# Attention: TensorE takes the 64-row score products of two steps together, and the other pieces are placed anew

## The chip, the cores and the metric

The kernel runs on one core of one Trainium2 chip. The metric is the device time of one execution in microseconds, as the median of several runs. The engines are called as in the profile: PE (TensorE, matrix products), PEld (its weight loads), DVE (VectorE), ACT (ScalarE), POOL (GpSimd) and SP (SyncE, which issues DMAs).

## The reference, cut to what matters

The input is 8 batches of 512 tokens with 256 features. A layer of causal attention with 16 heads of 16 features and a layer of routed experts run on the same normalised input. A second layer follows. The change lies in the attention of the first layer and in the small pieces that are woven into it.

```python
xn = _layernorm(x, axis=-1)
qkv = jnp.einsum('bsd,hde->bhse', xn, Wqkv) + bqkv[None, :, None, :]
q, k, v = jnp.split(qkv, 3, axis=-1)
score = jnp.einsum('bhsd,bhtd->bhst', q, k)
score = jnp.where(causal[None, None], score, -jnp.inf)
attn = jax.nn.softmax(score / jnp.sqrt(HEAD_DIM), axis=-1)
y = jnp.einsum('bhst,bhtd->bhsd', attn, v)
out = transpose_and_reshape(y) @ Wout + bout
...
scores = jax.nn.softmax(xn @ gate_w.T, axis=-1)      # router: two of eight experts for each token
```

## The kernel before

`mix_phase` holds the attention, its projections and the router. It takes the first 480 us of the profiled span. Each engine runs a program of its own, written out in order, and the engines meet on semaphores only. All of them walk the same steps: 8 batches, 16 heads in each, `U = 3` steps in a head. This makes 48 steps in a batch and 384 in all. In the loops `s` is the head counted over all batches, `at` is the step within its batch (0 to 47), and `i` is the step within its group of four heads (0 to 11). A batch has four groups. Two steps that begin with an even number are called a pair below (0 and 1, 2 and 3, and so on).

What PE does in a step:

- `scores_k` (L996, L999, L1000) makes a third of the scores of the next head, with the keys as rows, in one of two PSUM banks. It waits until `exps` of ACT (L583) has read what stood in that bank two steps earlier. A contraction has 49 rows.
- `scores_q` (L972, then two mask products L976 and L977) makes scores with the queries as rows, two groups ahead, only to take their maxima. Its results go to three banks in turn. `maxima` of DVE (L798) reads them, one unit in each step, and unit `i` waits until the maxima of unit `i - 3` are taken. A contraction has 48 or 64 rows.
- Each of these two uses one half of the 128 rows of the array, and in a step they use opposite halves, so that they run at the same time.
- The other pieces use all 128 rows. `turn_maxima` (L982) transposes the maxima of a finished group. DVE copies them to `max_rows` (L805), ACT issues two small DMAs that bring them into `q_stack` (`send_max`, L598, at `AT_SEND`, i = 4), and the first `scores_k` of the next group, at i = 9, waits for them. `values` (L1014) multiplies the exponentials with V in three parts, `turn_out` (L1024) transposes the result, and `divide` of DVE (L775, L777) scales it. `x_transposes` (L895), `q_products`, `k_products`, `v_products` and `logits` (all in `three_products`, L154 to L156) prepare the next batch. `out_transposes` (L1034) and `out_products` (L154 to L156) finish the batch before. `rank_sums` (L949, L950) belongs to the router.

At which step a piece stands is written in tables: `AT_X_T`, `AT_OUT_T`, `Q_STEPS`, `K_STEPS`, `PROJ_STEPS`, `V_STEPS`, `AT_LOGITS`, `AT_VALUES`, `AT_TURN` for PE, and `AT_STATS`, `AT_NORM`, `AT_RANKS` and others for DVE and POOL. ACT and DVE take their part of a piece one or two steps after PE (`at - 1`, `at - 2`). DVE also does `norm_stats` (L658, L666), `normalise` (L676), `residual` (L789), `x_low` (L683), `k_low` (L687), `out_low` (L784), `v_bias` (L695) and the router's small steps (L716 to L766), all in one order with the maxima.

The rows of Q and K of the next batch make a round trip through memory: ACT, POOL and DVE write `qk_hi` and `qk_lo`, SP stores them (`store_slots`, L371) and loads the stacks when the stores have landed (`fetch_heads`, L400). The first half of the heads is needed by `scores_q` at step 24 of the batch before, the second half at step 0 of the batch itself. After the loop of batch 0, SP also issues one store of zeros of 4 MB (`y_routed_dram`, L436), behind `store_xn(2)`, which waits for the last `normalise` of that batch.

## Time and profile before

| | us |
|---|---|
| median of 3 runs | 1220.95 (1220.65 to 1225.09) |
| the profiled execution | 1231.83 |
| its span, from first to last instruction | 1230.1 |
| PE busy in it | 1122.1 |
| DVE busy in it | 898.4 |
| ACT busy in it | 685.9 |
| POOL busy in it | 522.9 |

The profiled execution is one of its own, 10.9 us above the median. Its span leaves out 1.7 us. Times of a stretch are read from it; differences are carried to the median as they are. Matrix products are pipelined. A row of PE gives when a product starts and a modelled end, and the distance from start to start is what it costs in a stream. Rows of a timeline merge equal instructions that follow each other.

### The profile page before, as it was taken

Reading aid. Unit: us, or ns where it says so; the run is one execution under the profiler, and the core shown is the slowest. Engines: PE = TensorE matmul, PEld = TensorE weight load, DVE = VectorE, ACT = ScalarE, POOL = GpSimd, SP = SyncE. Lnnn points to the kernel's source line nnn. Section 1 sums busy time; section 2 is a strip of 40 time slices with the busy share of each in tenths; the row PEclk is TensorE's granted clock in tenths of the full one; section 3 lists DMA queues with packets and bytes.
Section 4 is the critical chain, followed back from the end, with each engine's and each line's share of the span. In section 5 each row is a group of like instructions: output and inputs, shape, how many; then the busy total and the mean of one; then the engine's idle time right before and its main releaser. Section 6 shows DMA issues by size and latency. Waiting matters only on the chain. (4 is left out here: it accounts for less than half of the span.)

```text
span 1230.1 us, 27639 instructions
## 1 busy us (share of the span) xinstructions
PE 1122.1 (91%) x9352; PEld 730.6 (59%) x9353; DVE 898.4 (73%) x2247; ACT 685.9 (56%) x1463; POOL 522.9 (43%) x752
## 2 busy tenths in 40 slices
PE   3889889999899887999899999997999999999998
PEld 2444444445454433888799888885556556556555
DVE  4769688887988663887566676675877877877866
ACT  2256466565665462656565666664654654654653
POOL 6124234242432221946344344433447447447424
PEclk8589999999999887999899999998999999999999
DMA  5437433344533402666232444443232322322312
GB/s 155 117 79 226 109 104 91 101 109 102 117 88 87 105 18 66 190 215 186 85 128 81 118 122 142 148 135 105 99 90 74 113 82 78 114 77 81 99 35 69
DMA packets 105783, 133.60 MB, mean 109 GB/s; under 512 B 11616, under 2 KB 93472, under 8 KB 104672
## 3 DMA queue, kind: packets, MB, share of 16 engines
q1 hardware_dynamic: 97760, 113.47, 31.9%
q0 software_dynamic: 6912, 18.88, 5.5%
q8 instruction: 50, 0.82, 0.3%
q14 instruction: 37, 0.30, 0.1%
q10 hardware_dynamic: 1024, 0.13, 0.1%
HBM read 84.70 MB, written 47.58 MB: 108 GB/s over the span
## 5 line engine op out<-in xcount | busy, mean ns | idle before, releaser
L583 ACT ACTIVATE p<-bank 128x384 f32<-128x384 f32 (+1 forms) x384 | 196.5, 526 | 184.5 <-PE bank L996 125.2
L798 DVE TENSOR_REDUCE neg_max<-bank 128x1 f16<-128x512 f32 (+3 forms) x384 | 223.0, 598 | 76.7 <-PE bank L977 74.2
L473 POOL TENSOR_SCALAR_AFFINE_SELECT p<-p 128x256 f32<-128x256 f32 x256 | 104.5, 413 | 259.2 <-ACT p L583 256.9
L972 PE MATMUL bank<-k_stack,q_stack 48*128 48x384 f16 (+3 forms) x512 | 140.0, 324 | 15.2 <-DMA k_stack<-qk_dram 13.0
L1444 POOL DMA_INDIRECT fetched<-xn_dram,token_now x80 | 80.5, 1006 | 42.9 <-POOL token_now L1440 30.7
L1014 PE MATMUL bank<-p,v_aug 128*32 128x512 f32 (+3 forms) x1024 | 97.9, 481 | 0.8 <-DVE o_rows L777 0.8
L996 PE MATMUL bank<-q_stack,k_stack 49*128 49x512 f16 (+1 forms) x256 | 90.2, 379 | 8.3 <-DMA q_stack<-max_rows 6.6
L2084 POOL TENSOR_TENSOR he_lo<-he_sq,he_hi 128x512 f16<-128x512 f32 x64 | 79.9, 1269 | 36.6 <-ACT he_hi L2173 36.6
L2073 POOL TENSOR_TENSOR up_lo<-up_sq,up_hi 128x512 f16<-128x512 f32 x32 | 43.8, 1399 | 121.3 <-ACT up_hi L2130 121.3
L1528 ACT ACTIVATE a<-xbank,b 128x256 f32<-128x256 f32 (+1 forms) x126 | 58.6, 468 | 52.8 <-PE xbank L156 49.2
L1616 DVE TENSOR_TENSOR h_lo<-h,h_hi 128x256 f16<-128x256 f32 x159 | 67.9, 430 | 25.8 <-ACT h_hi L1537 25.0
L154 PE MATMUL ybank<-l_xT_hi,pack_hi 128*128 128x512 f16 x208 | 79.7, 383 | 3.9 <-DVE up_sq L2287 2.1
L996 PEld LDWEIGHTS bank<-q_stack,k_stack 49*128 49x128 f16 x256 | 21.0, 94 | 100.8 <-ACT p L583 50.7
L976 PE MATMUL bank<-mask_cols,mask_rows 64*128 64x64 bf16 (+1 forms) x384 | 80.8, 211 | 0.0
L155 PE MATMUL ybank<-l_xT_lo,pack_hi 128*128 128x512 f16 x208 | 79.5, 382 | 0.0
L156 PE MATMUL ybank<-l_xT_hi,pack_lo 128*128 128x512 f16 x208 | 79.4, 382 | 0.0
L977 PE MATMUL bank<-mask_cols,mask_rows 64*128 64x64 bf16 (+1 forms) x384 | 78.9, 206 | 0.0
L1535 ACT ACTIVATE h<-prod 128x256 f32<-128x256 f32 x159 | 64.9, 408 | 24.4 <-DVE prod L1610 18.6
L1610 DVE SCALAR_TENSOR_TENSOR prod<-xbank,b,a 128x256 f32<-128x256 f32 (+1 forms) x126 | 58.5, 477 | 24.4 <-ACT a L1528 19.8
L156 PE MATMUL ybank<-pack_hi,up_lo 128*128 128x256 f16 x256 | 69.8, 273 | 0.0
L154 PE MATMUL ybank<-pack_hi,up_hi 128*128 128x256 f16 x256 | 69.8, 273 | 0.0
L155 PE MATMUL ybank<-pack_lo,up_hi 128*128 128x256 f16 x256 | 69.8, 273 | 0.0
(347 smaller groups left out, 3495.4 us busy)
## 6 DMA issues: line engine op xcount, KB each, us to landing
w_bc<-wT_dram SPq DMA_DIRECT2D x8, 2048.0 KB, 8.3
y_routed_dram<-y SPq DMA_DIRECT2D x37, 256.0 KB
qk_dram<-qk_hi SPq DMA_DIRECT2D x64, 128.0 KB
w<-in_w SPq DMA_DIRECT2D x10, 704.0 KB, 6.8
q_stack<-qk_dram SPq DMA_DIRECT2D x30, 192.0 KB, 4.1
k_stack<-qk_dram SPq DMA_DIRECT2D x30, 192.0 KB, 4.6
pack<-in_pack SPq DMA_DIRECT2D x12, 342.0 KB, 4.2
xr<-in_x SPq DMA_DIRECT2D x8, 512.0 KB, 3.9
```

Source lines behind the costliest of these rows:

```text
L154: pe.matmul(out, hi_a(c), hi_b(c), start=first and x == 0, stop=False)
L155: pe.matmul(out, hi_a(c), lo_b(c), start=False, stop=False)
L156: mm = pe.matmul(out, lo_a(c), hi_b(c), start=False, stop=last and x == n - 1)
L473: pool.affine_select(out=diagonal, in_=diagonal, pattern=[[0, 2], [1, P]], compare_op=ALU.is_ge, fill=0.0, base=0, channel_multiplier=-1). ...
L583: act.activation(p32[:, s // GH % 2, s % GH, cols], s_bank[(U * s + n) % S_BANKS][:, 0:cols.stop - cols.start], ACT.Exp).then_inc(p_exp.se ...
L798: dve.tensor_reduce(to, a_bank[c % A_BANKS][:, 0:len(pairs) * w].rearrange("p (x w) -> p x w", w=w), AX.X, ALU.max, negate=True).then_inc( ...
L972: pe.matmul(to[:, at * w:(at + 1) * w], q_stack[stack, u, pair0 + h, j * P:(j + 1) * P], k_stack[stack, u, pair0 + h, 0:w], start=at == 0, ...
L976: pe.matmul(blocks[:, :, j * P:j * P + HALF], mask_rows[half, HALF:HALF + P], cols, start=False, stop=False)
L996: mm = pe.matmul(to[:, 0:S - n * P], k_stack[rows, u, pair, n * P:(n + 1) * P], q_stack[rows, u, pair, n * P:S], start=True, stop=True)
L1014: mm = pe.matmul(out_bank[VW * h:VW * (h + 1), k * P:S], v_aug[:, b % 2, k, GH * (g % NG) + h, :], p32[:, g % 2, h, P_OFF[k]:P_OFF[k] + S ...
L1444: pool.indirect_dma_start(fetched[:, u, half, :], None, dram["xn"], bass.IndirectOffsetOnAxis(token_now[:, u, half:half + 1], 0)).then_inc ...
L2084: pool.tensor_tensor(he_lo[:, e, :], he_sq[:, e % EB, :], he_hi[:, e, :], ALU.subtract).then_inc(he_lo_s.sem, 1)
```

## The change

PE now does `scores_k` and `scores_q` of step v, then both of step v + 1, and after them the other pieces of v and of v + 1. `turn_maxima` moves from between `scores_k` and `scores_q` of i = 2 to the end of the other pieces of i = 1, and `turn_out` now stands ahead of `values`. The programs of ACT, DVE and POOL keep their form, but the tables that place the pieces have new numbers. Of these, `AT_NORM` goes from 42 to 45 to 31, 32, 35 and 36, `AT_STATS` from 38 and 39 to 26 and 27, `AT_XB` from 46 to 38, five of the six steps of `AT_RANKS` from 16 to 24 to 37 to 43, and the second half of `K_STEPS` from 27 and 28 to 30 and 32. No instruction is added or taken away.

```diff
-AT_X_T, AT_OUT_T, AT_LOGITS = (0, 2), (14, 16), 38
+AT_X_T, AT_OUT_T, AT_LOGITS = (0, 2), (15, 18), 44
...
-AT_VALUES, AT_COPY, AT_TURN, AT_DIVIDE = {5: (0,), 6: (1,), 8: (3, 2)}, 11, 1, 2
+AT_VALUES, AT_COPY, AT_TURN, AT_DIVIDE = {4: (0,), 6: (1,), 8: (3, 2)}, 11, 0, 2
+PAIR = 2
...
-            for s in range(NB * NH):
...
-                    if s + 1 < NB * NH:
-                        scores_k(s + 1, n)
-                    if i == TURN_BEFORE and group(s) <= GROUPS:
-                        turn_maxima(group(s) - 1)
-                    if group(s) < GROUPS:
-                        scores_q(group(s), i)
...
+            def scores(v):
+                s, n = v // U, v % U
+                if s + 1 < NB * NH:
+                    scores_k(s + 1, n)
+                if group(s) < GROUPS:
+                    scores_q(group(s), U * (s % GH) + n)
+
+            def others(v):
...
+                if i + 1 == TURN_BEFORE and group(s) <= GROUPS:
+                    turn_maxima(group(s) - 1)
+
+            for v in range(0, NB * NH * U, PAIR):
+                for of in range(PAIR):
+                    scores(v + of)
+                for of in range(PAIR):
+                    others(v + of)
```

PE, batch 0, third group, steps 30 and 31 (i = 6 and 7), before. L996 is `scores_k`, L972, L976 and L977 are `scores_q`, L1014 is `values`, and L154 begins a piece of `v_products`:

```order
L996 MATMUL bank<-q_stack,k_stack 128x512
L972 MATMUL bank<-k_stack,q_stack 128x512
L976 MATMUL bank<-mask_cols,mask_rows 128x64
L977 MATMUL bank<-mask_cols,mask_rows 128x64
L1014 MATMUL bank<-p,v_aug 32x384 x4
L996 MATMUL bank<-q_stack,k_stack 128x384
L972 MATMUL bank<-k_stack,q_stack 128x512
L976 MATMUL bank<-mask_cols,mask_rows 128x64
L977 MATMUL bank<-mask_cols,mask_rows 128x64
L154 MATMUL bank<-wqkv_hi,xT_hi 128x256
```

The same two steps after (the new file has each of these lines one number later):

```order
L997 MATMUL bank<-q_stack,k_stack 128x512
L973 MATMUL bank<-k_stack,q_stack 128x512
L977 MATMUL bank<-mask_cols,mask_rows 128x64
L978 MATMUL bank<-mask_cols,mask_rows 128x64
L997 MATMUL bank<-q_stack,k_stack 128x384
L973 MATMUL bank<-k_stack,q_stack 128x512
L977 MATMUL bank<-mask_cols,mask_rows 128x64
L978 MATMUL bank<-mask_cols,mask_rows 128x64
L1015 MATMUL bank<-p,v_aug 32x384 x4
L155 MATMUL bank<-xT_hi,wqkv_hi 128x512
```

The scores of both steps stand together, and `values` and the piece of `k_products` that now has its place here (L155) follow them.

DVE, batch 1, from the third group's copy of turned maxima, before. L805 is that copy, L775 and L777 are `divide`, and the L798 rows are maxima:

```order
L805 CAST max_rows<-bank 16x128
L798 TENSOR_REDUCE neg_max<-bank 128x1
L775 RECIPROCAL row_sum<-bank 128x16
L777 TENSOR_TENSOR o_rows<-bank,row_sum 128x4x64
L798 TENSOR_REDUCE neg_max<-bank 128x2 x2
L798 TENSOR_REDUCE neg_max<-bank 128x1 x2
L687 SCALAR_TENSOR_TENSOR qk_lo<-bank,bqk,qk_hi 128x512
```

The same place after (step 26 of batch 1 on), where L659 and L667 are `norm_stats` and L790 is `residual`:

```order
L806 CAST max_rows<-bank 16x128
L799 TENSOR_REDUCE neg_max<-bank 128x1
L776 RECIPROCAL row_sum<-bank 128x16
L778 TENSOR_TENSOR o_rows<-bank,row_sum 128x4x64
L659 BN_STATS stats<-xr 128x6 x2
L799 TENSOR_REDUCE neg_max<-bank 128x2
L790 TENSOR_TENSOR x<-bank,xb 128x512
L659 BN_STATS stats<-xr 128x6 x2
L667 BN_AGGR mv<-stats 128x2 x4
L799 TENSOR_REDUCE neg_max<-bank 128x2
```

`norm_stats` came here from the fourth group, and `residual`, which stood right before the copy, now stands behind two maxima.

## Rows read from the trace of the kernel before

**Rows 1.** The page, its first part: busy time, share, instructions of each engine.

```profile
PE 1122.1 (91%) x9352; PEld 730.6 (59%) x9353; DVE 898.4 (73%) x2247; ACT 685.9 (56%) x1463; POOL 522.9 (43%) x752
```

**Rows 2.** Stretches: from:to, length, PE, PEld, DVE, ACT, POOL busy, clock, DMA.

```profile
117.74:136.70 18.96, 14.79 (x130) 7.71 (x129) 12.32 (x32) 7.73 (x16) 3.66 (x9) 0.91 0.57 144
160.82:212.60 51.78, 47.70 (x487) 24.45 (x486) 43.94 (x117) 31.29 (x64) 18.62 (x38) 1.00 0.41 103
173.75:188.37 14.62, 13.00 (x129) 7.12 (x128) 11.97 (x32) 7.73 (x16) 3.50 (x9) 1.00 0.40 86
201.80:206.30 4.50, 4.16 (x63) 2.14 (x62) 4.38 (x16) 1.91 (x4) 1.22 (x4) 1.00 1.03 172
256.00:258.00 2.00, 2.00 (x10) 0.19 (x11) 1.91 (x9) 0.49 (x1) 0.59 (x3) 0.51 0.61 77
```

**Rows 3.** Timeline of PE, steps 32 to 36: start, length, line, names, form.

```profile
299.91 0.86 PE L1014 MATMUL bank<-p,v_aug 128*32 128x128 f32 x16
300.70 0.39 PE L996 MATMUL bank<-q_stack,k_stack 49*128 49x512 f16 x1
...
300.93 0.19 PE L976 MATMUL bank<-mask_cols,mask_rows 64*128 64x64 bf16 x1
300.96 0.19 PE L977 MATMUL bank<-mask_cols,mask_rows 64*128 64x64 bf16 x1
301.08 0.28 PE L154 MATMUL bank<-wqkv_hi,xT_hi 128*128 128x256 f16 x1
...
301.63 0.27 PE L156 MATMUL bank<-wqkv_hi,xT_lo 128*128 128x256 f16 x1
301.84 0.33 PE L996 MATMUL bank<-q_stack,k_stack 49*128 49x384 f16 x1
...
304.08 0.39 PE L996 MATMUL bank<-q_stack,k_stack 49*128 49x512 f16 x1
...
304.74 0.66 PE L1024 MATMUL bank<-identf,o_cols 128*128 128x128 f32 x4
```

**Rows 4.** Waits of PE from 160.82 to 212.60: total, times, longest.

```profile
PE bank L999 <- ACT p L583: 1.6, 4, 0.5
PE bank L1034 <- DVE tot L753: 1.0, 1, 1.0
PE bank L154 <- DVE xT_lo L683: 0.6, 1, 0.6
PE bank L154 <- DVE oT_lo L784: 0.6, 1, 0.6
```

**Rows 5.** Waits of DVE from 160.82 to 212.60.

```profile
DVE neg_max L798 <- PE bank L977: 5.8, 14, 0.8
```

**Rows 6.** Groups of DVE by form, 201.64 to 253.33: busy, mean ns, idle before.

```profile
L798 DVE TENSOR_REDUCE neg_max<-bank 128x1 f16<-128x512 f32 x16 | 10.9, 689 | 3.7 <-PE bank L977 3.7
```

**Rows 7.** Timeline of SP: the round trip of the first half of heads.

```profile
278.25 0.57 SPq L371 DMA_DIRECT2D qk_dram<-qk_lo  x1
...
282.65 0.44 SPq L400 DMA_DIRECT2D k_stack<-qk_dram  x1
```

**Rows 8.** Issues from 150 to 400: size, median to landing.

```profile
k_stack<-qk_dram SPq DMA_DIRECT2D x18, 192.0 KB, 4.6
```

**Rows 9.** Timeline of PE: step 24 begins.

```profile
289.94 0.39 PE L996 MATMUL bank<-q_stack,k_stack 49*128 49x512 f16 x1
```

**Rows 10.** Timeline of ACT: a send of maxima.

```profile
295.23 1.29 ACTq L598 DMA_DIRECT2D q_stack<-max_rows  x2
```

**Rows 11.** Packets from 295.89 to 297.30, queue of the sends: packets, MB, share.

```profile
q10 hardware_dynamic: 32, 0.00, 1.8%
```

**Rows 12.** Waits of PE from 40 to 470, those for DMAs.

```profile
PE bank L996 <- DMA q_stack<-max_rows: 6.6, 3, 3.8
...
PE bank L972 <- DMA k_stack<-qk_dram: 4.3, 2, 2.6
```

**Rows 13.** Timeline of SP: the store of zeros.

```profile
102.93 0.65 SPq L436 DMA_DIRECT2D y_routed_dram<-zeros_f  x1
```

More of the change, by code:

```diff
@@ L1069, in _ @@
                 scores_k(0, n)
-            for s in range(NB * NH):
-                b, h = s // NH, s % NH
-                for n in range(U):
-                    at, i = U * h + n, U * (s % GH) + n
-                    if s + 1 < NB * NH:
-                        scores_k(s + 1, n)
-                    if i == TURN_BEFORE and group(s) <= GROUPS:
-                        turn_maxima(group(s) - 1)
-                    if group(s) < GROUPS:
-                        scores_q(group(s), i)
-                    if s >= GH:
-                        if i in AT_VALUES:
-                            values(s // GH - 1, AT_VALUES[i])
-                    if s >= 2 * GH and i == AT_TURN:
-                        turn_out(s // GH - 2)
-                    if at == AT_RANK_SUMS:
-                        rank_sums(b)
-                    if b >= 1:
-                        if at in AT_OUT_T:
-                            out_transposes(b - 1, AT_OUT_T.index(at), turn_o[AT_OUT_T.index(at)])
-                        for g, half in part_at(PROJ_STEPS, at):
-                            out_products(b - 1, g, half, turn_p[g])
-                    if b + 1 < NB:
-                        if at in AT_X_T:
-                            x_transposes(b + 1, AT_X_T.index(at), turn_x[AT_X_T.index(at)])
-                        for m, c in part_at(Q_STEPS, at):
-                            q_products(b + 1, m, c, turn_q[m])
-                        for m, c in part_at(K_STEPS, at):
-                            k_products(b + 1, m, c, turn_k[m])
-                        for g, half in part_at(V_STEPS, at):
-                            v_products(b + 1, g, half, turn_v[g])
-                        if at == AT_LOGITS:
-                            logits(b + 1)
@@ new lines, in scores @@
+            def scores(v):
[5 more added lines that the diff above has]
+            def others(v):
+                s, n = v // U, v % U
+                b, at, i = s // NH, U * (s % NH) + n, U * (s % GH) + n
+                if s >= 2 * GH and i == AT_TURN:
+                    turn_out(s // GH - 2)
+                if s >= GH and i in AT_VALUES:
+                    values(s // GH - 1, AT_VALUES[i])
+                if at == AT_RANK_SUMS:
+                    rank_sums(b)
+                if b >= 1:
+                    if at in AT_OUT_T:
+                        out_transposes(b - 1, AT_OUT_T.index(at), turn_o[AT_OUT_T.index(at)])
+                    for g, half in part_at(PROJ_STEPS, at):
+                        out_products(b - 1, g, half, turn_p[g])
+                if b + 1 < NB:
+                    if at in AT_X_T:
+                        x_transposes(b + 1, AT_X_T.index(at), turn_x[AT_X_T.index(at)])
+                    for m, c in part_at(Q_STEPS, at):
+                        q_products(b + 1, m, c, turn_q[m])
+                    for m, c in part_at(K_STEPS, at):
+                        k_products(b + 1, m, c, turn_k[m])
+                    for g, half in part_at(V_STEPS, at):
+                        v_products(b + 1, g, half, turn_v[g])
+                    if at == AT_LOGITS:
+                        logits(b + 1)
+                if i + 1 == TURN_BEFORE and group(s) <= GROUPS:
+                    turn_maxima(group(s) - 1)
```

6 lines of the change are left out of this document (3 added, 3 removed).

## The prediction, made before the result was known

> **What bounds the kernel now.** I read the page first: PE is busy for 91% of the span, DVE for 73%, ACT for 56% [rows 1]. Shares over the whole span mix the attention with the expert layers, which the change doesn't touch, so the next view is the table of stretches. The attention runs in a fixed rhythm. Batches 2 to 6 take 51.8 us each, and in one of them PE is busy for 47.7 and DVE for 43.9 [rows 2]. The reader is to see two engines near their limit, with DVE only four microseconds below PE, and ACT far away with 31.
>
> The third view is the timeline of PE, read by the distance between starts, since a modelled end lies beyond the next start. Two mask products of 64 rows start 0.03 us apart, but from the second one to a product of 128 rows are 0.12 us. Products of 128 rows with 256 columns start 0.11 us apart (five distances between 301.08 and 301.63), but from the last of them to a 64-row product are 0.21 us [rows 3]. So each change between 64 and 128 rows costs 0.09 to 0.10 us, in both directions. PE changes 84 times in such a batch by its written order: 8.0 us of the 51.8.
>
> The fourth view is the waits. In a batch PE stands still for 3.8 us in the rows [rows 4]. Modelled ends hide some 0.17 us in each of the seven waits (a 64-column product has a length of 0.19, while the next starts 0.03 later [rows 3]), so the true sum is about 5. DVE waits for PE's scores for 5.8 us [rows 5], so its own work lies between its busy 43.9 and 51.8 - 5.8 = 46.0. I take 45, since small waits within the router's chain belong to it. PE's own work is 51.8 - 5, about 46.7.
>
> **The change part by part.** *Fewer changes of rows.* Walking both loops, a middle batch goes from 84 changes to 46, the first from 62 to 40, the last from 51 to 37, all eight from 617 to 353. A middle batch saves 38 x 0.095 = 3.6 us of PE work, and ends at 43.1. Most of it lies on the path, since PE is the busier engine. The fourth group gives least of this: there many steps had no other piece, and their scores stood together already, as in step 36, whose two score steps take 0.66 us until `turn_out` starts, where one step alone took 0.38 [rows 3]. A rule of the Trainium skill would size it otherwise. "TensorEngine Tiling (Array Packing)", Key Properties, says that a change of the tiling mode drains the engine, and "TensorE: Matmul & The Clock Gate", Single matmul latency, puts the fixed part of a lone product at about 166 ns; if each change cost that, a batch would gain 6.3 us and not 3.6. The trace shows 0.09 to 0.10, and the sum goes by it.
>
> *DVE's work is unchanged.* 45 a batch now stands above PE's 43, and DVE becomes the busier engine. Three banks let PE run three maxima ahead and no more, and a pair takes two of them at once, so what counts is how much DVE has to do within a pair. A maximum of 512 columns takes 0.69 us, some 0.6 from start to start [rows 6]. A pair of steps on PE is 0.6 to 0.7 of scores [rows 3], 0.8 of a last `values` part, and 0.65 for a projection piece that follows another 128-row piece (0.76 alone, less one change) [rows 3]: about 2.1, and 1.6 where `values` stands alone (its first part scaled to 512 columns: 1.0). I walked one batch with such lengths.
> - First group: `q_products` needs `x_low`, which stands behind a maximum and `divide`. PE arrives some 0.25 us earlier than now, so the 0.6 of [rows 4] becomes 0.9. In steps 10 to 13 DVE has the router's weights, `k_low` and the first of the ranks besides four maxima. PE waits 0.6 at `turn_maxima` and 1.2 at the next `scores_q`.
> - Second group: the wait for `tot` (1.0) goes, because that copy moves to step 13 and `out_transposes` to 18. Of the wait for `oT_lo` (0.6) remain 0.2.
> - Third group: `norm_stats` and `residual` meet at steps 26 and 27. The stretch 201.80 to 206.30 holds today's same spot, with `divide`, `norm_stats` and three maxima, and DVE is busy for 4.38 of 4.50 there [rows 2]. With one more `residual`, PE's pair of 2.1 and the pair of 1.6 after it don't cover it: 1.0 of waiting at i = 7.
> - Fourth group: `v_bias` and ranks take its first pairs, 0.5 of waiting. Its last pair has no other piece, and the next scores find the banks of ACT and DVE full: 0.8. This takes the place of the 1.6 that now end with ACT's exponentials [rows 4].
>
> *Round trips through memory.* The first half of the heads: from the last store to the last issue of a load are 4.4 us [rows 7], to its landing 4.6 more [rows 8], so it is there at 287.3, and 288.2 if the last of four lands a microsecond late. Step 24 begins at 289.94 [rows 9]. The slack is 1.7 to 2.6 us, and the way from `k_low` to step 24 shrinks by about 2.5: from 0 to 0.8 of waiting, of which I take 0.8, because DVE does `k_low` later in the pair. The second half starts four steps later than now (`K_STEPS` ends at 32) and is needed at step 48: 0 to 0.8, and I take 0.4.
>
> The waits add up to 0.9 + 0.6 + 1.2 + 0.2 + 1.0 + 0.5 + 0.8 + 0.8 + 0.4 = 6.4, and some run together: DVE catches up while PE waits for a load. I take 5.6. A batch is then 43.1 + 5.6 = 48.7, which is 3.1 less than now.
>
> *The store of zeros* (one DMA of 4 MB) is issued at 102.93, at the start of batch 1 [rows 13]. It delays all transfers behind it, and steps 14 to 26 of that batch take 18.96 us [rows 2]. The same twelve steps take 14.62 in the next batch [rows 2], so the store costs 4.3, and the DMA wait of up to 2.6 is its visible part [rows 12]. With `normalise` done at step 36, the store is issued some nine steps earlier and falls into the fourth group of batch 0, where only a send of maxima is in its way. Cost there: 0 to 2.5 (two sends have waited 2.8 us or less beside one of 3.8 [rows 12]), I take 1.9. Net 2.4.
>
> **Sum.** Batches 2 to 6: 5 x 3.1 = 15.5. Batch 1: 3.1 + 2.4 = 5.5. Batch 0: 22 changes, 2.1, of which part is lost to its own load wait at step 24: 1.5. Batch 7: 14 changes, 1.3, but its transfers for the shared expert set part of the pace: 0.5. Together 23. The profiled execution would go from 1231.8 to 1209, the median from 1221 to **1198**.
>
> **The rivals.** *A, as above.* 1188 to 1208.
>
> *B, DVE's gaps close further.* Waits are shared better than my walk has them, and a batch takes DVE's 45 plus a microsecond: 46. That is 5.8 a batch, 6 x 5.8 = 35, with 2.4 and 2 for the rest 39: 1182. For it: DVE waits 5.8 us today [rows 5]. Against it: its work is lumpy.
>
> *C, DVE sets the pace pair by pair.* If in each pair the slower engine decided, a batch would cost 53.1 today and 51.6 after by the same lengths. Today's batch is 51.8, near that. A gain of 1.5 a batch, some 10 in all, with 2.4 for the store: 1208, and up to 1219 if the store finds a worse place. "TensorEngine Tiling (Array Packing)", PSUM Bottleneck, in the Trainium skill, warns of this: what the array gains does not speed up the reading of PSUM.
>
> *D, slower: the sends come too late.* Now the second send of maxima is issued about 0.65 after 295.23 [rows 10], and its first use is at 300.70 [rows 3], 4.8 us later. After the change `scores_k` of i = 9 stands ahead of the `values` part of i = 8, and the sends still wait for the exponential of i = 4. Two pairs and one score step (1.6 + 2.1 + 0.35) less 1.2 for that exponential and the second issue leave 2.8. Undisturbed, all 32 packets have gone 1.4 us after the second issue [rows 11], so it fits. But the loads of the second half now fall on the same stretch. Each microsecond beyond 2.8 costs 31 us in 31 groups. It turns the whole change into a loss from a landing of about 3.6 on. At 4.0 it would be 1198 + 37 = 1235.
>
> *E, the clock.* From 256 to 258 the granted clock was 0.51 [rows 2], the lower level of 1.2 GHz, after PE had waited in the fourth group. Waits will now stand elsewhere. A stretch at half the clock loses half its length where PE sets the pace. Four falls of 3 us in a batch would lose 6.0, nearly twice the gain of 3.1: 1221 + 6 x 2.9 - 3 = 1235. It decides from some 6 us at the lower level in each batch on.
>
> That the change doesn't do what it says is excluded by the written order of PE, which shows the scores of two steps together.
>
> **How the numbers follow.** A 0.55, B 0.12, C 0.22, D 0.06, E 0.05. About 0.5%, 6 us, is what a measurement of this kernel can tell from no change. A, B and two thirds of C are below 1215: 0.81 faster. The rest of C is the same: 0.10. D, but for its small end, and E: 0.09 slower, with a remainder of C. The range takes A, the nearer half of B and most of C: 1184 to 1215.
>
> **What would show it.** Right: 46 changes of rows in a middle batch at the same 0.09 to 0.10, a batch near 48.7, DVE busy for 90% of it, PE waiting for `neg_max` (hardly seen now), no wait for `tot`, no long load wait in batch 1. For B: a batch near 46 with DVE above 94%. For C: one above 50. For D: waits of `scores_k` for `q_stack<-max_rows` in each group. For E: a granted clock below 0.95 in the stretches of middle batches. My sum would be wrong if a change of rows cost less in the new order than in the old, or if the walk missed a lump of DVE.

## The result, and the profile after

The changed kernel takes 1233.06 us in the median of 7 runs (1229.11 to 1247.72), the kernel before 1224.9 in 7 runs beside it (1220.63 to 1230.75). One of the 7, the 1247.72, was a slow run that the ratio leaves out; without it the median is 1231.7. The ratio is 1.006, with a 95% interval of 1.0031 to 1.009. The forecast was 1198, a gain of 23 us; the change lost about 7. Measured again on another chip the ratio was 1.0025 (1.0003 to 1.0047).

The profiled execution of after has a time of 1229.11 and a span of 1227.3. The busy times, from its page, beside [rows 1]:

```profile
PE 1112.4 (91%) x9352; PEld 731.8 (60%) x9353; DVE 915.3 (75%) x2247; ACT 679.6 (55%) x1463; POOL 523.9 (43%) x752
```

PE is busy for 10 us less and DVE for 17 us more, although no instruction of either was added. That second number is the first hint.

The next view cuts both spans at the same four points of the program (start, `turn_maxima` in the fourth group of batch 1, the same in batch 6, and the last `turn_maxima`, in batch 7). Columns as in [rows 2]. Before:

```profile
0.00:149.86 149.86, 117.01 (x964) 59.49 (x965) 101.72 (x262) 65.70 (x128) 51.00 (x105) 0.83 0.50 137
149.86:408.95 259.09, 239.45 (x2432) 122.33 (x2431) 219.78 (x587) 156.88 (x315) 93.13 (x186) 0.99 0.40 100
408.95:451.90 42.95, 35.76 (x330) 17.62 (x329) 29.23 (x84) 20.23 (x42) 9.65 (x24) 0.80 0.23 57
451.90:1230.10 778.20, 729.89 (x5630) 531.13 (x5629) 547.66 (x1319) 443.10 (x979) 369.16 (x439) 0.98 0.36 109
```

After:

```profile
0.00:143.30 143.30, 109.34 (x951) 57.93 (x952) 104.94 (x261) 64.77 (x128) 52.55 (x107) 0.85 0.52 140
143.30:416.17 272.87, 242.14 (x2431) 125.89 (x2430) 231.62 (x576) 151.62 (x315) 91.76 (x184) 0.94 0.39 96
416.17:452.93 36.76, 33.70 (x343) 17.90 (x342) 28.89 (x83) 20.26 (x42) 9.61 (x25) 0.86 0.31 72
452.93:1227.30 774.37, 727.25 (x5632) 530.07 (x5631) 549.83 (x1329) 442.93 (x978) 369.98 (x439) 0.98 0.35 109
```

The first stretch gained 6.6 us and the third 6.2. The last, which is all but untouched by the change, differs by 3.8; so much can be noise of a single execution. The whole loss is in the second, five batches in rhythm: 272.9 instead of 259.1, or 54.6 a batch instead of 51.8, where 48.7 was forecast. DVE's extra 12 us lie there too, and the granted clock is 0.94 instead of 0.99. These are single executions. The changed kernel again (e12) takes 272.55 in this stretch. The kernel before, but for the place of its sends (e10, as fast as before), takes 262.75 there, so of the 13.8 some 4 can be the choice of the execution.

Four such groups, after (a first one from batch 2; the second, third and fourth from batch 4):

```profile
158.78:171.57 12.79, 11.33 (x113) 5.43 (x112) 11.47 (x39) 8.73 (x18) 4.42 (x10) 1.00 0.25 73
280.20:293.70 13.50, 12.16 (x125) 7.10 (x125) 10.55 (x22) 7.39 (x15) 3.38 (x9) 1.00 0.46 90
293.70:306.16 12.46, 11.57 (x119) 5.95 (x118) 11.85 (x29) 7.81 (x16) 5.46 (x11) 1.00 0.30 90
306.16:321.72 15.56, 12.54 (x135) 6.45 (x134) 13.13 (x31) 6.37 (x14) 5.15 (x10) 0.89 0.59 133
```

Before, the fourth group took 10.96 us and now it takes 15.56, with PE standing still for 3 of them. Its cause is on DVE. The timeline of DVE there, after (L757 is the second half of `router_ranks`, an addition of 8 columns; L806 the copy to `max_rows`):

```profile
306.28 0.42 DVE L799 TENSOR_REDUCE neg_max<-bank 128x2 f16<-128x256 f32 x1
306.62 2.63 DVE L757 TENSOR_TENSOR route_run<-route_run,tot 128x8 f32<-128x8 f32 x2
309.28 0.28 DVE L806 CAST max_rows<-bank 16x128 f16<-16x128 f32 x1
```

And of POOL at the same time (L461 is `x_bias`):

```profile
306.52 2.35 POOL L461 TENSOR_TENSOR xb<-xr,bout_row 128x1024 f32<-128x1024 f32 x1 [0.31 <-DVE xn L677]
```

Two additions of 8 columns take 2.63 us, and the copy starts 0.4 us after `x_bias` has ended. The groups of DVE and POOL by form, with the same columns as [rows 6], first for a middle batch of before:

```profile
L460 POOL TENSOR_TENSOR xb<-xr,bout_row 128x1024 f32<-128x1024 f32 x1 | 2.3, 2349 | 2.0 <-DVE xn L676 2.0
L756 DVE TENSOR_TENSOR route_run<-route_run,tot 128x8 f32<-128x8 f32 x4 | 0.8, 188 | 0.1
```

The same batch after:

```profile
L757 DVE TENSOR_TENSOR route_run<-route_run,tot 128x8 f32<-128x8 f32 x4 | 2.9, 728 | 0.1
L677 DVE TENSOR_SCALAR xn<-xr,mv,rstd 128x256 f32<-128x256 f32 x5 | 2.8, 555 | 0.0
L461 POOL TENSOR_TENSOR xb<-xr,bout_row 128x1024 f32<-128x1024 f32 x1 | 2.3, 2342 | 0.3 <-DVE xn L677 0.3
```

`x_bias` itself lasts as long as before; only the small addition grows, by 2.1 us. The Trainium skill, "SBUF — State Buffer", SBUF: two separate sides, has the rule: DVE and GpSimd share a pair of ports, whichever starts first holds it for its whole instruction, and an operation of DVE with two SBUF inputs is locked out by one of GpSimd that reads SBUF. Both are such operations, and the rows agree: the one that starts 0.1 us later waits for the other's end.

What PE waits for in a middle batch, after (total, times, longest), beside [rows 4]:

```profile
PE bank L997 <- ACT p L584: 2.2, 4, 0.9
PE bank L973 <- DVE max_rows L806: 1.3, 1, 1.3
PE bank L155 <- DVE xT_lo L684: 1.0, 1, 1.0
PE bank L997 <- DMA q_stack<-max_rows: 0.8, 1, 0.8
PE bank L973 <- DVE neg_max L799: 0.4, 1, 0.4
PE bank L983 <- DVE neg_max L799: 0.2, 1, 0.2
PE bank L1015 <- DVE o_rows L778: 0.2, 1, 0.2
```

The second row is the addition above. The first is another cause. The timeline of ACT in the second group (L584 exponentials, L599 the two sends, L575 `out_high`):

```profile
283.18 0.49 ACT L584 ACTIVATE p<-bank 128x384 f32<-128x384 f32 x1 [1.13 <-PE bank L997]
283.19 1.29 ACTq L599 DMA_DIRECT2D q_stack<-max_rows  x2
284.58 0.60 ACT L575 ACTIVATE oT_hi<-bank 128x512 f16<-128x512 f32 x1 [0.91 <-issue]
285.07 1.40 ACT L584 ACTIVATE p<-bank 128x384 f32<-128x384 f32 x3
```

And of PE beside it:

```profile
284.36 0.39 PE L997 MATMUL bank<-q_stack,k_stack 49*128 49x512 f16 x1
...
285.61 0.33 PE L997 MATMUL bank<-q_stack,k_stack 49*128 49x384 f16 x1 [0.80 <-ACT p L584]
```

ACT starts the exponentials of i = 4, which run until 283.67. Its queue issues the two DMAs from 283.19 on, for 1.29 us, and ACT starts nothing new until 284.58, 0.91 us after the exponentials end. Then it takes `out_high`, and only at 285.07 the exponentials of i = 5. PE wants that bank for `scores_k` of i = 7. With single steps there was a piece between the scores of 6 and 7; in a pair they follow each other, and PE waits 0.80.

### The profile page after: what moved, and what is told of

Its sections match the earlier page's. It is cut to its first block and busy times, and to the rows that moved or that the text cites. A ratio compares the mean times of both kernels' runs of the same rounds, so it can differ in the third digit from the quotient of the medians.

```text
span 1227.3 us, 27621 instructions
## 1 busy us (share of the span) xinstructions
PE 1112.4 (91%) x9352; PEld 731.8 (60%) x9353; DVE 915.3 (75%) x2247; ACT 679.6 (55%) x1463; POOL 523.9 (43%) x752
## 3 DMA queue, kind: packets, MB, share of 16 engines
q10 hardware_dynamic: 1024, 0.13, 0.1%
## 5 line engine op out<-in xcount | busy, mean ns | idle before, releaser
L584 ACT ACTIVATE p<-bank 128x384 f32<-128x384 f32 (+1 forms) x384 | 188.7, 527 | 176.7 <-PE bank L997 87.1
L799 DVE TENSOR_REDUCE neg_max<-bank 128x1 f16<-128x512 f32 (+3 forms) x384 | 219.8, 598 | 59.0 <-PE bank L978 56.0
L973 PE MATMUL bank<-k_stack,q_stack 48*128 48x384 f16 (+3 forms) x512 | 133.7, 328 | 22.8 <-DMA k_stack<-qk_dram 9.4
L997 PE MATMUL bank<-q_stack,k_stack 49*128 49x512 f16 (+1 forms) x256 | 93.3, 385 | 24.2 <-ACT p L584 15.5
L1015 PE MATMUL bank<-p,v_aug 128*32 128x512 f32 (+3 forms) x1024 | 102.9, 502 | 1.7 <-DVE o_rows L778 1.7
L2081 POOL TENSOR_TENSOR up_lo<-up_sq,up_hi 128x512 f16<-128x512 f32 x32 | 43.9, 1398 | 121.0 <-ACT up_hi L2138 121.0
L155 PE MATMUL ybank<-l_xT_hi,pack_hi 128*128 128x512 f16 x208 | 79.5, 382 | 3.7 <-DVE up_sq L2295 2.1
L977 PE MATMUL bank<-mask_cols,mask_rows 64*128 64x64 bf16 (+1 forms) x384 | 81.4, 212 | 0.0
L155 PE MATMUL ybank<-pack_hi,up_hi 128*128 128x256 f16 x256 | 69.8, 273 | 0.0
```

The lines of the kernel that those rows point to most:

```text
L155: pe.matmul(out, hi_a(c), hi_b(c), start=first and x == 0, stop=False)
L584: act.activation(p32[:, s // GH % 2, s % GH, cols], s_bank[(U * s + n) % S_BANKS][:, 0:cols.stop - cols.start], ACT.Exp).then_inc(p_exp.se ...
L799: dve.tensor_reduce(to, a_bank[c % A_BANKS][:, 0:len(pairs) * w].rearrange("p (x w) -> p x w", w=w), AX.X, ALU.max, negate=True).then_inc( ...
L973: pe.matmul(to[:, at * w:(at + 1) * w], q_stack[stack, u, pair0 + h, j * P:(j + 1) * P], k_stack[stack, u, pair0 + h, 0:w], start=at == 0, ...
L977: pe.matmul(blocks[:, :, j * P:j * P + HALF], mask_rows[half, HALF:HALF + P], cols, start=False, stop=False)
L997: mm = pe.matmul(to[:, 0:S - n * P], k_stack[rows, u, pair, n * P:(n + 1) * P], q_stack[rows, u, pair, n * P:S], start=True, stop=True)
```

## The experiments

There are sixteen runs, in four sets; e12 repeats the changed kernel and e13 repeats e9. Kernels of one set ran on one chip beside the kernel before. Runs e1 to e4 are one set (before: 1229.4 us), e5 to e8 the next (1269.86, a slower chip), then e9 to e12 (1229.85) and e13 to e16 (1229.91). All diffs are against the changed kernel unless said otherwise.

**e1: x_bias back at 46.**

```diff
-AT_STATS, AT_RSTD, AT_NORM, AT_XB = (26, 27), 29, (31, 32, 35, 36), 38
+AT_STATS, AT_RSTD, AT_NORM, AT_XB = (26, 27), 29, (31, 32, 35, 36), 46
```

> The changed kernel with one number put back: AT_XB is 46 again and not 38, so that POOL adds its 1024-column x_bias eight steps later. Theory 1 (POOL and DVE shut each other out of SBUF: in the changed kernel the first of two 8-column adds of the ranks, L757, takes 2273 ns instead of 155 while x_bias runs from 306.52 to 308.87 on POOL, and scores_q of i = 4 then waits 1.32 us for the copy behind it): the add takes its 0.16 us again, the wait of 1.32 for max_rows is gone, the granted clock no longer falls in the fourth group, and a middle batch goes from 54.4 us to 51 to 52; ratio to before about 0.99. Theory 2 (the sends of maxima, which hold ACT for 1.3 us while the scores of two steps wait for its exponentials, cost the gain): the batch stays at 54, and only the 1.32 moves elsewhere; ratio 1.00 to 1.01.

Measured: 1222.7 us, ratio 0.9946 (0.9912 to 0.998). L757 is back at a mean of 188 ns and the wait for `max_rows` is gone; its two quickest middle batches take 51.3 and 51.5. A loss of 0.6% became a gain of 0.5%. But the five average 53.2, and the clock did not come back as expected: it is 0.94 in this stretch, as in after. The waits for ACT stay, and in the fourth group PE now waits 0.75 to 1.9 us for the sends to land, so the next wait in line took a part.

**e2: the ranks moved away instead.**

```diff
-AT_RANKS = (13, 37, 39, 40, 41, 43)
+AT_RANKS = (13, 39, 40, 41, 42, 43)
```

> The changed kernel with the ranks of the router placed two steps later (13, 39, 40, 41, 42, 43 for 13, 37, 39, 40, 41, 43); x_bias stays at 38. DVE then has only sources in PSUM while x_bias runs. Theory 1: the same relief as from moving x_bias, a middle batch of 51 to 52 and a ratio of about 0.99, with no wait of 1.3 for max_rows. Theory 2: no more than 0.5 us of a batch. If this helps and moving x_bias doesn't, it was the place of the ranks in DVE's order and not the overlap.

Measured: 1227.69 us, ratio 0.999 (0.9957 to 1.0022). Here too the wait for `max_rows` is gone, with `x_bias` left where it was. So that wait comes from the coincidence of the two, not from the place of either. In the ratio this is weaker: the interval lies just below the first one of after (1.0031 to 1.009) and overlaps with that of e12 (1.0003 to 1.0047). Waits for landing of 0.95 to 2.04 us in four fourth groups eat more of the gain than in e1, and three of five batches take 53.7 us or more.

**e3: pairing alone**, with all tables of before: the changed kernel with the numbers on the minus side of the diff in the section on the change, and `PAIR = 2`.

> PE takes the scores of two steps together as in the changed kernel, but every table is that of before. It parts the order of PE from the new places. Theory 1: nothing runs on POOL beside DVE's two-source work, so a part of the saved changes of rows is kept: fewer changes of rows than 84 in a batch, batch 50 to 51.5, ratio 0.985 to 1.0. Theory 2: the exponentials wait for the sends as in the changed kernel (0.8 to 0.9 us in each of two or three groups), ratio 1.0 to 1.015.

Measured: 1214.83 us, ratio 0.9866 (0.981 to 0.9923). Three of its five middle batches take 50.7 to 50.9, with a short fall of the clock in each. One of them:

```profile
141.30:192.05 50.75, 46.67 (x488) 25.08 (x487) 43.46 (x118) 30.89 (x64) 18.52 (x37) 0.97 0.43 106
```

PE changes rows 46 times in it, as in after. Pairing alone is better than the whole change by 1.9%. With the pairing in place, the tables are what lost.

**e4: the new tables alone.**

```diff
-PAIR = 2
+PAIR = 1
```

> The tables of the changed kernel, but PE takes the steps one at a time (PAIR = 1). Theory 1: the collision at steps 37 and 38 is there without any pairing, L757 takes over 2 us, and the kernel is slower than before: 1.01 to 1.02, about as slow as or slower than the changed kernel, since no change of rows is saved. Theory 2: without pairing the sends cost nothing, ratio 0.99 to 1.0.

Measured: 1226.14 us, ratio 0.9985 (0.9954 to 1.0016). The tables lose nothing without the pairing. `x_bias` starts just behind the addition, and the L757 before it lasts 382 ns. But the tables should have gained: they crowd pieces into fewer steps, so PE changes rows 64 times in a middle batch here and not 84. At a clock of 0.97 a batch takes 52.3 to 52.7, against 52.27 in before, so the 1.9 us of 20 changes at 0.095 went into other waits. So the loss belongs to neither half of the change alone: pairing alone gained 1.3%, the tables alone 0.2% (within the noise), both together lost 0.3 to 0.6%.

**e5 and e6: x_bias at 46 and the sends one step earlier (e5), and `normalise` moved off POOL's `q_low` too (e6).**

```diff
-AT_STATS, AT_RSTD, AT_NORM, AT_XB = (26, 27), 29, (31, 32, 35, 36), 38
+AT_STATS, AT_RSTD, AT_NORM, AT_XB = (26, 27), 29, (33, 34, 35, 36), 46
...
-AT_SEND = 4
+AT_SEND = 3
```

(In e5 `AT_NORM` stays.)

> The changed kernel with AT_XB back at 46 and, new against that, AT_SEND = 3: ACT issues the two sends of maxima one step earlier, ahead of the exponentials and evacuations of i = 4. Theory 2 (the sends hold ACT for 1.3 us just where two score steps wait for it, and land too late for i = 9 in the fourth group): scores_k's waits for ACT of 0.3, 0.8 and 0.9 us in three groups and for the landing (1.1 to 1.9 us in the fourth group) shrink to a third, and a middle batch goes from 51.6 (without falls of the clock) to 49 to 50; ratio to before 0.975 to 0.985, against 0.995 for the kernel without this. Theory 3 (what is lost after moving x_bias is the granted clock alone): the waits go, but the time only moves by what the clock regains; if the clock stays near 0.94 the ratio stays above 0.99.

> As the run before, with AT_NORM (33, 34, 35, 36) in place of (31, 32, 35, 36), so that DVE's first normalise doesn't meet POOL's q_low of step 30. Theory 1 (two-port or two-source work of DVE and POOL shut each other out): normalise, L677, takes its 0.40 us and not 1.15; up to 0.7 us less in a batch, of which 0 to 0.7 is on the path, ratio lower by 0 to 0.004. Rival: the 0.75 was hidden behind PE all along, no difference in time.

Measured: e5 1250.12 us, ratio 0.9832 (0.9777 to 0.9887); e6 1248.02, ratio 0.9824 (0.9792 to 0.9857). The waits of `scores_k` for ACT and for `q_stack` are down to 0.24 us a batch. At full clock a batch takes 49.6 to 50.0; with the falls of the clock the five average 50.6 (e5) and 50.9 (e6). In e6 L677 is back from 555 to about 400 ns, and the time did not move: that collision was real, but hidden.

**e7 and e8: pairing alone with the sends at 3 (e7), and the first of the ranks at 13 (e8)**, both against e3.

```diff
-AT_RANKS = (15, 16, 18, 19, 20, 24)
+AT_RANKS = (13, 16, 18, 19, 20, 24)
...
-AT_SEND = 4
+AT_SEND = 3
```

> The tables of before, PE in pairs, and AT_SEND = 3. Theory 2: with the old tables ACT has no evacuation in the step of the send, and the waits for exponentials were small already (0.4 in one group), so little is gained, 0 to 1 us in a batch, ratio 0.980 to 0.987. If the gain is as large as with the new tables, the send itself and not the evacuation beside it is what holds the pair.

> As the run before, and the copy of the rank sums (the first of AT_RANKS) at step 13 instead of 15, as the changed kernel has it, with the other ranks left where they were. DVE then has the sums before out_transposes asks for them: the wait for tot of 0.44 us goes, and perhaps some of the wait for oT_lo of 0.7. In the second group the clock fell in each of the profiled batches of the paired kernel with the old tables (0.89 over 15.5 us); if waits bring the clock down, it should stay up here more often. 0 to 1.5 us less in a batch; ratio 0.970 to 0.985.

Measured: e7 1255.77 us, ratio 0.9872 (0.9819 to 0.9925); e8 1250.93, ratio 0.9846 (0.977 to 0.9922). Both lie within the interval of e3: with the old tables one step earlier buys nothing that can be measured. That it is the evacuations behind the sends that make the difference in the new tables fits this, but no run moved them alone. Two batches at full clock take 48.75 in e8, where before and e10 take 51.7: the old tables could nearly be kept.

**e9 and e13: the repaired kernel.** The waits left in e6 were `x_low` (1.02 a batch) and the third group's maxima behind `norm_stats` and `residual` (0.75 to 1.1). Three numbers were moved by a step or two for them, together, so that no run parts their shares:

```diff
-Q_STEPS, ... = ((3, 6), (26, 27)), ...
+Q_STEPS, ... = ((4, 6), (26, 27)), ...
...
-AT_STATS, AT_RSTD, AT_NORM, AT_XB = (26, 27), 29, (31, 32, 35, 36), 38
+AT_STATS, AT_RSTD, AT_NORM, AT_XB = (28, 29), 31, (33, 34, 35, 36), 46
...
-AT_SEND = 4
+AT_SEND = 3
```

> The changed kernel with AT_XB 46, AT_SEND 3, AT_NORM 33 to 36, and also the first of Q_STEPS at 4 instead of 3, AT_STATS 28 and 29, AT_RSTD 31. By the theory that each remaining wait is a place where a piece of DVE stands right behind its partner: the wait of q_products for x_low (1.02 in each batch) falls below 0.5, the wait of scores_q for neg_max in the third group (0.75 to 1.1) falls below 0.4, a batch at full clock takes 48 to 49, and the ratio to the kernel before is 0.970 to 0.980. By the rival that DVE is so near its limit that a wait removed in one place comes back in the next: batches stay at 49.5 to 50.5 and the ratio at 0.980 to 0.985.

> The repaired kernel of before once more (AT_XB 46, AT_SEND 3, AT_NORM 33 to 36, AT_STATS 28 and 29, AT_RSTD 31, first of Q_STEPS at 4), as the measure for the three that go with it. Every theory: 0.967 to 0.975 of the kernel before, batches of 48.7 to 50.2 us, no wait of PE above 0.5 us in a middle batch.

Measured: 1193.8 us, ratio 0.9711 (0.9669 to 0.9753), and once more 1193.77, ratio 0.9699 (0.9651 to 0.9747). It beats both kernels. The same four cuts, e13:

```profile
0.00:133.74 133.74, 107.61 (x951) 57.60 (x952) 100.29 (x260) 64.47 (x128) 52.38 (x107) 0.87 0.55 150
133.74:380.67 246.93, 237.46 (x2431) 125.52 (x2431) 215.97 (x577) 150.48 (x315) 91.52 (x184) 0.95 0.44 106
380.67:415.11 34.44, 32.14 (x343) 16.99 (x342) 28.85 (x83) 19.86 (x42) 9.56 (x25) 0.90 0.31 77
```

Against before it gained 16.1 us up to the first cut, 12.2 in five middle batches and 8.5 in batch 7. A middle batch is 49.4 on average, and its four groups (first to fourth) are:

```profile
194.04:205.85 11.81, 11.43 (x113) 5.31 (x112) 11.14 (x39) 8.75 (x18) 4.73 (x10) 1.00 0.42 124
256.34:270.38 14.04, 13.31 (x126) 7.36 (x126) 10.55 (x22) 7.34 (x15) 3.23 (x8) 0.88 0.42 84
270.38:281.81 11.43, 11.43 (x119) 5.84 (x118) 10.77 (x28) 7.71 (x16) 5.45 (x11) 1.00 0.31 98
281.81:293.20 11.39, 10.81 (x134) 6.36 (x133) 11.01 (x32) 6.28 (x14) 5.11 (x10) 1.00 0.64 137
```

Beside the groups of after: 1.0 less in the first (the wait for `x_low`), 1.0 less in the third (the wait behind ACT), 4.2 less in the fourth (the addition, the landing, and the clock). The second is 0.5 longer, for the clock falls there.

**e10: the kernel before with the sends at 3** (`AT_SEND = 3`, nothing else).

> The kernel before with AT_SEND 3 alone. In it the scores stand singly, so the two issues of ACT fall beside a step of PE that has other work. By the theory that the pairing exposes the sends: ratio 0.997 to 1.003. By the rival that an earlier send helps any order of the work, paired or not: 0.985 to 0.995, since four groups of eight batches would each gain 0.4 us.

Measured: 1231.8 us, ratio 1.0018 (0.9989 to 1.0047). An earlier send is worth nothing in the unpaired order.

**e11: the changed kernel with the sends at 3**, `x_bias` left at 38.

> The changed kernel with AT_SEND 3 alone, AT_XB left at 38. By the theory of two separate causes: the waits of scores_k for the exponentials of i = 5 (0.3 to 0.9 in three groups) and for q_stack (about 1 in the fourth) go, the wait for max_rows of 1.3 in the fourth group stays, and the ratio is 0.987 to 0.997, between the changed kernel (1.006) and the one with both repairs (0.983). By the rival that the long wait for max_rows and the clock falls behind it are the whole loss: above 1.000.

Measured: 1225.35 us, ratio 0.9984 (0.9946 to 1.0023). The waits behind ACT are gone (0.24 is the longest), the wait of 1.32 for `max_rows` is there in each batch. In the third group a wait of 0.75 to 1.1 for `neg_max` appears in the place of the one that went. The waits for the sends to land were expected to go too, but two of five fourth groups have one, of 2.4 and 1.1. The five middle batches take 273.4 us, no less than in after; the profiled execution is quicker in batches 0, 1 and 7 instead. So this run shows that the waits behind ACT go, but not that they alone cost time.

**e12: the changed kernel again.**

> The changed kernel once more, beside the other three on the same chip. Every theory: 1.003 to 1.009 of the kernel before, with the wait for max_rows of 1.3 us in the fourth group of each middle batch and about six clock falls between batch 1 and batch 7. If the ratio differs by more than 0.005 from the first measurement, the size of each cause depends on the chip.

Measured: 1232.47 us, ratio 1.0025 (1.0003 to 1.0047), with the same waits for DVE and ACT at the same places. The wait for the sends to land, though, is in none of its five middle batches, and they take 272.55 us all the same, with about 41 us at the lower clock level where after had 31.

**e14: the repaired kernel without pairing** (`PAIR = 1`).

> The repaired kernel with PAIR 1: its tables, but the scores of each step stand alone, so that PE changes its rows 84 times in a middle batch instead of 46. By the theory of the prediction (0.095 us for a change, PE the busier engine): 38 x 0.095 = 3.6 us more in each middle batch, about 27 us more in all, so 0.990 to 0.998 of the kernel before. By the rival that the new places alone bring the gain: within 0.005 of the repaired kernel, 0.967 to 0.978.

Measured: 1229.83 us, ratio 0.9985 (0.9951 to 1.0019), against 0.9699 for e13 beside it. The pairing is worth 36 us in these tables, more than the 27 expected. The expectation had one number wrong: PE changes rows 64 times in a middle batch of this kernel, as in e4, and not 84. That is 18 changes more than the paired one, which at 0.095 would be 1.7 us. The five middle batches:

```profile
142.16:416.07 273.91, 255.23 (x2434) 129.09 (x2431) 222.46 (x574) 155.59 (x315) 91.83 (x183) 0.90 0.39 96
```

27 us above e13, and the clock is 0.90 instead of 0.95. Two batches with the same clock of 0.97 in both kernels take 51.3 to 51.5 here and 48.7 to 48.9 there: 2.6 us a batch, or 13 in five. PE's waits account for all of it: they are 3.1 us in 9 places of such a batch here and 1.3 to 1.6 in 4 or 5 there, and with the 0.17 that a modelled end hides of each the difference is about 2.5. So in these tables the pairing pays by fewer waits, and the rows don't show the 1.7 of saved changes. The other half goes with the clock: some 55 us at the lower level in the five batches, against 24 in e13.

**e15: the repaired kernel with x_bias back at 38.**

> The repaired kernel with AT_XB back at 38, which puts x_bias of GpSimd again beside the ranks of DVE. By the theory: one add of 8 columns lasts over 2 us again, PE waits 1.0 to 1.4 for max_rows in the fourth group of seven batches, and the clock falls behind it: 8 to 17 us more, a ratio 0.007 to 0.014 above that of the repaired kernel. By the rival that this was hidden and only moved the clock's falls about: below 0.004 more.

Measured: 1216.02 us, ratio 0.988 (0.9834 to 0.9926): 22.3 us above e13, more than expected. The group by form, over the whole attention, shows the addition again (mean 188 ns in before), and the middle stretch is 18.7 us longer than in e13:

```profile
L757 DVE TENSOR_TENSOR route_run<-route_run,tot 128x8 f32<-128x8 f32 x32 | 20.4, 639 | 0.6
```

```profile
136.99:402.58 265.59, 247.89 (x2431) 127.81 (x2431) 227.59 (x577) 150.35 (x315) 91.78 (x184) 0.92 0.40 99
```

PE's waits for `max_rows` are 1.3 in each of six batches, 7.9 in all.

**e16: the repaired kernel with the sends back at 4.**

> The repaired kernel with AT_SEND back at 4. By the theory: scores_k of i = 6 waits 0.3 to 1.2 for the exponentials of i = 5 in three groups, and the fourth group waits about 1 for q_stack: 1.5 to 2.5 a batch, 12 to 18 us in all, a ratio 0.010 to 0.015 above the repaired kernel. By the rival that the two issues only mattered because other waits had made ACT late: below 0.004 more.

Measured: 1218.01 us, ratio 0.9891 (0.9853 to 0.993): 24.2 us above e13, twice what was expected. The waits of PE in one of its middle batches at full clock (51.20 us):

```profile
PE bank L997 <- ACT p L584: 2.4, 4, 0.9
PE bank L997 <- DMA q_stack<-max_rows: 1.8, 1, 1.8
```

and in a middle batch of e13:

```profile
PE bank L973 <- DVE neg_max L799: 0.6, 2, 0.4
PE bank L155 <- DVE oT_lo L785: 0.2, 1, 0.2
PE bank L997 <- ACT p L584: 0.2, 1, 0.2
```

(Its `scores_k` that waits for ACT is that of i = 7; the expectation said 6.) The profiled execution of e16 is 30 us longer than that of e13, and 20 of them lie in the five middle batches. So each of the two causes, put back alone, costs 22 to 24 us in the median. With both and three smaller ones the changed kernel was 38.7 us above the repaired one (e12 and e9, the same chip), less than their sum. That one is caught up while PE waits for the other would explain it, but is not shown.

## Why the prediction was wrong, point by point

**The saving of row changes** was right in its count and its price, not in what reached the time. PE changes 46 times in a middle batch of after, as walked, and the distances are those of [rows 3]. With the old tables, where pairing alone takes 84 changes to 46, a batch of e3 takes 50.75 with some 3 us at the lower clock, so about 49.5 without (by the price below), 2.2 less than before; at full clock e7 takes 49.1 and e8 48.75, 2.6 and 2.9 less. Forecast were 3.6 of saved work and 3.1 after new waits. In the new tables 20 of the 38 changes are saved by the tables and only 18 by the pairing (e4, e14), and neither part is seen in the time as such. That a change of the tiling mode drains TensorE, as the Trainium skill says ("TensorEngine Tiling (Array Packing)", Key Properties), agrees with the gap of 0.09 to 0.10 us at each change; the price of a whole lone product for it, 6.3 us a batch, is not borne out.

**"DVE's work is unchanged. 45 a batch"** is the first step that failed. DVE is busy for 231.6 in the middle stretch of after and for 216.0 in that of e13, 3.1 us a batch more for the same instructions: 2.1 of it the addition behind `x_bias`, 0.8 one `normalise` (1157 ns instead of 399) behind `q_low`. The durations of the walk were those of before, taken at places where POOL did something else. The diff moved `AT_XB` and `AT_RANKS` onto each other, and the prediction gave `AT_XB` no term at all. PE waits 1.3 + 0.2 us for it in each batch, and more by what follows: put back alone into the repaired kernel, it costs 22 us (e15).

**The sends.** Rival D priced their landing, with 2.8 us left and 0.06 of chance, and looked at every group. It came true in the fourth group alone: 0.4 to 1.1 us in three of five batches, and in none of e12. There the loads of the second half stand in the way, as it said. SP issues them from 307.92 on, ACT's sends follow at 309.58 (both after):

```profile
307.92 0.31 SPq L401 DMA_DIRECT2D q_stack<-qk_dram  x1
```

```profile
309.58 1.61 ACTq L599 DMA_DIRECT2D q_stack<-max_rows  x2
311.25 0.49 ACT L584 ACTIVATE p<-bank 128x384 f32<-128x384 f32 x1 [2.43 <-issue]
```

The 2.43 us between two exponentials of ACT are not all the issues': for the first 0.8 ACT waits for the copy that the addition has delayed (its end is at 309.56), then come the two issues. What no term and no rival had is that the two issues hold ACT, and this is the second step that failed; put back alone it costs 24 us (e16). The sum said that the waits for ACT's exponentials (1.6 in [rows 4]) would be replaced by 0.8; they are 2.2, of which 0.8 and 0.9 come at i = 7 in the second and third groups of this batch (0.9 to 1.2 in each third group, 0.8 to 1.1 in three of five second groups). The row needed was in [rows 10]: 1.29 us of ACT's queue, which was used only as a delay of the send and not as work of ACT.

**The clock.** Rival E had 0.05 of chance. The row that it rested on says little: ahead of 256 PE had waited 0.34 us, as it had at the same place of the four other batches of before, where no fall followed. It called 6 us in each batch decisive, and there were six, at a lower price than its half. In the middle stretch the lower level of 1.2 GHz was granted for about 30 us (twice the missing share of the batches' clocks, 0.91, 0.97, 0.97, 0.97 and 0.91), in before for some 3. What that costs is shown by three stretches of e15, the same twelve steps with the same work, at three levels:

```profile
271.43:284.27 12.84, 11.96 (x126) 7.02 (x126) 10.45 (x22) 7.28 (x15) 3.23 (x8) 1.00 0.47 91
218.45:232.48 14.03, 13.30 (x126) 7.61 (x126) 10.74 (x22) 7.35 (x15) 3.23 (x8) 0.88 0.41 85
163.96:179.57 15.61, 14.88 (x126) 7.92 (x126) 10.74 (x22) 7.34 (x15) 3.23 (x8) 0.78 0.33 76
```

A clock of 0.78 means 6.9 us at the lower level and costs 2.8; 0.88 means 3.4 and costs 1.2: about 0.38 us for each. A batch of before with one fall agrees: 52.27 us with 3.4 at the lower level, and 51.7 without. The 27 us more than in before would then cost 10 of the 13.8 that the stretch lost. In after the falls come mostly behind the long wait of the fourth group:

```profile
253.00:256.00 3.00, 1.62 (x16) 0.84 (x14) 2.93 (x5) 1.09 (x3) 2.52 (x3) 1.00 0.45 118
256.00:260.00 4.00, 3.77 (x23) 1.15 (x27) 3.79 (x13) 1.35 (x3) 0.41 (x1) 0.58 1.11 191
```

But the repaired kernel has a clock of 0.95 there too, with its falls in the second group and hardly a wait ahead of them, and e16 had two batches at 1.00 with a wait of 1.8 or 1.9 in each. Nor is the clock of before as steady as its one profile has it. The same stretch of e10, an order as fast as before:

```profile
149.90:412.65 262.75, 243.55 (x2431) 123.82 (x2431) 219.57 (x587) 156.95 (x315) 93.18 (x186) 0.97 0.39 98
```

That is 14 us at the lower level, so the surplus of after is 17 to 27 us and its cost 6 to 10. Over whole executions it is about 15 us: the median clock is 0.950 in the 10 runs of e12, 0.956 in the 25 of before beside them, and 0.9595 in the 4 of e9. What decides a fall was not settled. The clock is a part of the loss and not the whole: after and e13 differ by 26 us in this stretch, and by 7 us at the lower level.

**Adding up.** A middle batch of after took 54.6 where 48.7 was forecast. Taken apart as the prediction did it, the mean of the five is: waits in the rows 5.7, hidden in nine modelled ends 1.6, clock 2.3 (6 us by 0.38), and the rest, PE's own work, 45.0. Forecast were 5.6 of waits, nothing for the clock, and 43.1. So 1.7 of the 5.9 are waits, 2.3 the clock, and 1.9 work that was not saved. The waits were further off than that 1.7 says: the 1.3 behind the addition, some 1.5 behind ACT at i = 7 and some 0.6 for landing stand in no term, and what was forecast at steps 10 to 13, at the third group's i = 7 and for loads came small or not at all. The same reckoning gives PE 46.7 in each batch of before and 43.8 to 43.9 in the batches at full clock of e7 and e8, so pairing with the old tables saved 2.8 of the 3.6. Why PE's own work is 45.0 in after, and 45.2 to 45.8 in e13, is not shown; waits shorter than a modelled end would stand in it unseen.

**The hand walk**, place by place: `x_low` 0.9 forecast, 1.0 found. `oT_lo` 0.2, found 0.24. The wait for `tot` gone, as said. `turn_maxima` 0.6 and `scores_q` 1.2 at steps 10 to 13, found 0.24 or less and 0.4. The third group's 1.0 at i = 7 was hidden by ACT's wait and came out at 0.75 to 1.1 when that was removed (e5, e11). PE waiting for `neg_max`, a sign of being right, is 0.4 to 1.1 us a batch in after; where the pairing paid it is there (6.4 us in 13 places of e3's five batches). DVE busy for 90% of a batch: it is 85% in after, held time included, and 87% in e13.

**The store of zeros** was right. It is issued at 94.44 instead of [rows 13], and steps 13 to 25 of batch 1 take 13.2 us instead of 18.96. The fourth group of batch 0, where it falls now, takes 15.4 us, no more than the same group of the batches that follow, so the 1.9 set aside for it is not seen. Batches 0 and 1 together gained 6.6, where 7.0 was forecast (up to the first cut; in e12 9.0). **Batch 7** gained 6.2, where 0.5 was forecast. It holds the longest wait of [rows 12], 3.8 us for a send, with 10 us at the lower level right behind it. Of the 17 us at the lower level in this stretch 10 remain in after, and the longest wait there is 1.4. The prediction read that row as a price and did not ask whether the change would take it away.

**Rival C**, whose 53.1 and 51.6 stand without their working, would have had a batch at 51.6 and lies nearest among those that say faster, but it isn't what happened: no row of after shows PE waiting for `neg_max` pair by pair. The rival that came nearest was D, with E behind it, and both together had a chance of 0.11. The repaired kernel's ratio of 0.9705 would bring the median of 1221 to 1185, inside the range; but the range was given for the change as it was made.

## What to carry to other kernels

When a change moves a long operation of GpSimd, list what DVE does beside it in the new place, above all small additions with both inputs in SBUF: 8 columns cost 155 ns alone and 2.27 us behind another's lock. Count the issue of a DMA as work of the engine that issues it, 0.63 us each (the median of ACT's 64), and ask whose exponentials or copies stand behind it in the new order. When instructions are put closer together, every wait that a piece in between used to cover is a term of the sum, and time at the lower clock level is another. And take a second execution before a single profile is called the habit of a kernel: the share of the lower level and the waits for landing differed between two of the same kernel.

## What the runs showed of the hardware

- An addition of DVE with two SBUF inputs and one of POOL on 1024 columns exclude each other: the mean of L757 over the attention is 188 ns apart from POOL and 639 with seven such meetings (e15). A `TENSOR_SCALAR` of DVE with one SBUF tensor (L677) was held too, beside POOL's `q_low`.
- Two DMA issues take ACT's queue for 1.29 us, and ACT starts no instruction while they last (0.91 us idle behind an exponential that still ran).
- A microsecond at the lower clock level costs 0.35 to 0.40 us of a stretch (the three rows of e15), less than the 0.5 that PE alone would lose.
- Falls of the clock don't follow the total of waits: the repaired kernel waits least and still has 24 us at the lower level in five batches (27 in e9), where before had 3 and e10 14. Their places repeat: in both executions of the repaired kernel all five falls are in the second groups. How long they last doesn't.
